# Routing table of the second layer: the slots of items 12 to 15 summed by TensorE from one-hot marks, ranks moved up, other table entries spread

## The reference

```python
gates = softmax(flat @ Wgate)                       # flat: 4096 x 256
_, top_inds = top_k(gates, 2)
mask = zeros((N, E), bool).at[arange(N)[:, None], top_inds].set(True)
pos = cumsum(mask, axis=0) * mask - 1               # rank of a token within its expert
keep = (pos < capacity) & mask
exp_in = zeros((E, capacity, d)).at[e_flat, p_eff].set(flat[t_flat], mode='drop')
hmid = gelu(einsum('ecd,edf->ecf', exp_in, W1) + b1, approximate=False)
exp_out = einsum('ecf,efd->ecd', hmid, W2) + b2
moe = zeros((N, d)).at[t_flat].add(exp_out[e_flat, p_g] * gate)
return x + moe
```

## Time and profile before

| | |
|---|---|
| median of 3 runs | 1511.07 us (1511.07 to 1511.7) |
| the profiled execution itself | 1514.36 us, of which the span from first to last instruction is 1512.6 us |
| busy in the span: PE, DVE, ACT, POOL | 1397.3, 1063.2, 898.2, 651.4 us |
| mean granted TensorE clock | 0.963 of 2.4 GHz |
| end of item 15's attention to the first product of the second layer | 1098 to 1130.7 us |
| products of the second layer | 1130.7 to the end |

### The profile page before, as it was taken

How to read it: one execution, slowest core, us unless ns; L and a number is a source line. 1 busy time by engine, 2 the same in 40 slices (tenths; PEclk the granted TensorE clock), 3 DMA queues, 4 the chain that set the end, 5 groups by cost and what they waited for, 6 DMA issues and landing times.

```text
span 1512.6 us, 26340 instructions
## 1 busy us (share of the span) xinstructions
PE 1397.3 (92%) x9265; PEld 1190.9 (79%) x9265; DVE 1063.2 (70%) x2514; ACT 898.2 (59%) x2092; POOL 651.4 (43%) x624
## 2 busy tenths in 40 slices
PE   7987899999999999999999998998729999999997
PEld 5765789999999998777876776776518888888886
DVE  2998577777777776778897787885436666666654
ACT  5776355555555553378887887887626455465452
POOL 0222344344343414555556665553434435445333
PEclk9998899999999999999999999999759999999999
DMA  6421256666665633343453454442432443234212
GB/s 176 140 81 37 60 155 170 171 177 178 172 186 170 171 102 124 100 142 116 133 147 100 135 142 102 123 123 71 126 85 58 93 102 95 38 98 100 40 22 29
DMA packets 133587, 173.53 MB, mean 115 GB/s; under 512 B 20725, under 2 KB 105536, under 8 KB 133456
## 3 DMA queue, kind: packets, MB, share of 16 engines
q1 hardware_dynamic: 105296, 119.89, 24.4%
q0 software_dynamic: 28160, 51.96, 17.3%
HBM read 107.28 MB, written 42.08 MB: 99 GB/s over the span
## 4 chain that ended last, share of the span: by engine, by line
PE 74%; DVE 8%; issue 6%; DMA 5%; ACT 3%; POOL 2%; another core or an unknown queue 1%; SPq 1%; POOLq 0%; DVEq 0%; ACTq 0%
PE banks L941 33%; PE banks L1983 8%; PE banks L1470 5%; PE banks L1514 4%; DMA xe<-pooled,idx 4%; PE banks L1985 4%; PE banks L1567 4%; PE banks L1003 3%; PE banks L451 2%; PE banks L1527 2%; PE banks L1488 1%; PE banks L1529 1%; PE banks L1959 1%; DVE row_at L516 1%
## 5 line engine op out<-in xcount | busy, mean ns | idle before, releaser
L941 PE MATMUL banks<-hi_x,hi_w 128*128 128x320 f32 (+1 forms) x832 | 289.4, 348 | 9.9 <-DVE hidden L976 5.3
L941 PE MATMUL banks<-lo_x,hi_w 128*128 128x320 f32 (+1 forms) x832 | 287.6, 346 | 0.0
L941 PE MATMUL banks<-hi_x,lo_w 128*128 128x320 f32 (+1 forms) x832 | 287.6, 346 | 0.0
L882 POOL DMA_INDIRECT xe<-pooled,idx x160 | 159.1, 995 | 235.1 <-DVE hidden L976 104.4
L1618 ACT ACTIVATE PN<-banks,smax 128x256 f32<-128x256 f32 (+1 forms) x512 | 180.3, 443 | 11.9 <-DVE smax L1724 11.9
L1443 POOL DMA_INDIRECT got<-done,slot x128 | 125.6, 981 | 143.3 <-DVE smax L1724 71.4
L1983 PE MATMUL banks<-down_w,hi_h 128*128 128x512 f32 x512 | 183.8, 401 | 0.0
L1944 POOL DMA_INDIRECT out<-X,tab x64 | 100.1, 1565 | 187.1 <-DVE X L2048 157.7
L941 PEld LDWEIGHTS banks<-hi_x,hi_w 128*128 128x128 f32 x832 | 159.6, 192 | 25.1 <-issue 8.0
L941 PEld LDWEIGHTS banks<-hi_x,lo_w 128*128 128x128 f32 x832 | 159.3, 192 | 13.7
L941 PEld LDWEIGHTS banks<-lo_x,hi_w 128*128 128x128 f32 x832 | 159.7, 192 | 12.3
(11 more groups left out here) (194 smaller groups left out, 3299.7 us busy)
## 6 DMA issues: line engine op xcount, KB each, us to landing
w<-in_L_ffn_w SPq DMA_DIRECT2D x96, 256.0 KB
done<-res SPq DMA_DIRECT2D x31, 640.0 KB
BIG<-in_L_ffn_W SPq DMA_DIRECT2D x16, 1024.0 KB
QS<-parts_qk SPq DMA_DIRECT2D x48, 256.0 KB
KS<-parts_qk SPq DMA_DIRECT2D x96, 128.0 KB
mask<-in_c_masks SPq DMA_DIRECT2D x16, 257.0 KB, 2.9
pooled<-XF SPq DMA_DIRECT2D x16, 256.0 KB, 3.2
WS<-in_L_cond_W SPq DMA_DIRECT2D x16, 256.0 KB
```

The source lines that it names most:

```text
L882: e.indirect_dma_start(xe[:, n % NXE, i, :], None, pooled, bass.IndirectOffsetOnAxis(ap=idx0[:, n * NS0 + i:n * NS0 + i + 1], axis=0)).the ...
L941: last = e.matmul(o, a[i], b[j], start=start and k == 0, stop=stop and k == 2, skip_group_check=True)
```

## The change

The 16 entries of items 12 to 15 are no longer written to DRAM. For each of these items (m = 0 to 3) a step `mark` on DVE splits its 4 times 128 slots into lane (slot / 64) and column (slot mod 64), makes one-hot marks of both and multiplies the column marks by the pair's two values; a step `find` on PE sums four products of marks into PSUM bank 0, at [lane, value, column]. The table of the other 48 entries is loaded by SP before the end of attention (`table`), to `listed`; the new `dve_table1` adds both into `tab`. To make sums possible a token is stored as a float, less N, and an empty place is 0. The slot is now place times 8 plus expert, not expert times 1024 plus place.

The ranks of group 6 (items 12, 13) and of group 7 (item 14) move up in PE's order, and their slots in DVE's. The entries of items 10 to 13's rounds that are left are spread over the rounds by waits on the count of row maxima. A load of `lanes1` (the numbers 0 to 127) is new in SP's order.

```diff
-        np.tile(np.arange(E0) * CAP0 - S0, (P, 1)), np.tile(np.arange(E1) * CAP1 - S1, (P, 1))], 1)
+        np.tile(np.arange(E0) * CAP0 - S0, (P, 1)), np.tile(np.arange(E1) - S1, (P, 1))], 1)
-    token = (p[:, None] + P * np.arange(NT)[None, :]).astype(np.int32)
+    token = p[:, None] + P * np.arange(NT)[None, :] - N
...
+        if r.stride == 1:
+            e.tensor_tensor(r.sm[:, 0:n, :], pos, base, ALU.add).then_inc(*st.next())
+        else:
+            e.scalar_tensor_tensor(r.sm[:, 0:n, :], pos, float(r.stride), base, ALU.mult, ALU.add).then_inc(*st.next())
...
     POOL_ROUND = (
         ("qk", 1, 0), ("qk", 1, 1), ("got", 3, 0, 0), ("got", 3, 0, 1), ("got", 3, 0, 2), ("entry", -3, 0), ("base", -2),
-        ("got", 3, 0, 3), ("got", 3, 1, 0), ("norm", -1, 1), ("got", 3, 1, 1), ("norm", 2, 0), ("entry", -3, 1),
+        ("late", -3, 1), ("late", -3, 2), ("late", -3, 3), ("ahead", -2, 0), ("ahead", -2, 1), ("got", 3, 0, 3), ("got", 3, 1, 0), ("norm", -1, 1), ("got", 3, 1, 1), ("norm", 2, 0), ("entry", -3, 1),
...
     POOL_LAST = (
-        *(("entry", 13, i) for i in range(TB * K1)), *(("entry", 14, i) for i in range(R * K1)), ("norm", 15, 1),
-        *(("entry", 15, i) for i in range(TB * K1)), *(("entry", 16, i) for i in range(TB * K1)))
+        ("entry", 13, 2), ("entry", 13, 3), ("norm", 15, 1))
     SP_LAST = (
-        ("base", 13), ("normed", 14), ("load_w1", 0), ("load_w1", 1), ("base", 14), ("normed", 15), ("base", 15))
+        ("lanes", 0), ("base", 13), ("normed", 14), ("load_w1", 0), ("load_w1", 1), ("base", 14), ("table", 0), ("normed", 15),
+        ("base", 15))
...
+            elif step == "table":
+                e.wait_ge(s_xc, B)
+                e.wait_ge(s_fill1, 48)
+                e.wait_ge(s_scat1, 16 * NSC)
+                e.wait_ge(s_in1, LANES_IN)
+                e.dma_start(listed, table1.rearrange("(p c) w -> p c w", p=P)).then_inc(s_in1, 16)
...
+    entry_pace = {(b, i): (s_smax, 3 * NG * (b + 3) + n) for b in range(LATE, B - 4) for i, n in ((1, 1), (2, 4), (3, 6))}
+    entry_pace.update({
+        (12, 1): (s_smax, 3 * NG * 15), (12, 2): (s_lgs, 14), (12, 3): (s_smax, 3 * NG * 15 + 1), (13, 0): (s_smax, 3 * NG * 15 + 4),
+        (13, 1): (s_smax, 3 * NG * 15 + 7), (13, 2): (s_smax, 3 * NG * 15 + 10), (13, 3): (s_smax, 3 * NG * 15 + 12)})
...
+    def pe_find1(e, m):
+        if m == 0:
+            e.wait_ge(s_pn, exp_count(NG * B - 1, 0))
+        e.wait_ge(s_marked1, m + 1)
+        for q in range(NHOT):
+            last = e.matmul(found1(), lane_hot[m % 2][:, q, :], slot_hot[m % 2][:, q, :, :].rearrange("p v c -> p (v c)"),
+                            start=m == 0 and q == 0, stop=m == 3 and q == NHOT - 1, skip_group_check=True)
+        last.then_inc(s_found1, 1)
...
+    def dve_mark1(e, m):
...
+        slots = slot1[:, t, :].rearrange("p r k -> p (r k)")
+        e.tensor_scalar(lane, slots, NCOL.bit_length() - 1, None, ALU.logical_shift_right).then_inc(*st.next())
+        e.tensor_scalar(col, slots, NCOL - 1, None, ALU.bitwise_and).then_inc(*st.next())
+        e.wait_ge(st.sem, st.n)
+        e.tensor_tensor(col_hot, wide(lanes1[:, 0:NCOL], 1, [P, NHOT, NCOL]), wide(col, 2, [P, NHOT, NCOL]),
+                        ALU.is_equal).then_inc(*st.next())
+        e.tensor_tensor(lane_hot[m % 2], wide(lanes1, 1, [P, NHOT, P]), wide(lane, 2, [P, NHOT, P]), ALU.is_equal).then_inc(*st.next())
+        e.wait_ge(st.sem, st.n)
+        e.tensor_tensor(slot_hot[m % 2], wide(col_hot, 2, [P, NHOT, 2, NCOL]),
+                        wide(pair1[:, t, :, :].rearrange("p r k v -> p (r k) v"), 3, [P, NHOT, 2, NCOL]), ALU.mult).then_inc(s_marked1, 1)
+
+    def dve_table1(e):
+        e.wait_ge(s_in1, TABLE_IN)
+        e.wait_ge(s_found1, 4)
+        found = found1().rearrange("p (v c) -> p v c", v=2)
+        flat = tab[:, :, :, :].rearrange("p i e w -> p (i e) w")
+        e.scalar_tensor_tensor(flat[:, :, 0].bitcast(U32), found[:, 0, :], float(N), listed[:, :, 0], ALU.add, ALU.add).then_inc(r1.s_slots, 1)
+        e.tensor_tensor(flat[:, :, 1], found[:, 1, :], listed[:, :, 1], ALU.add).then_inc(r1.s_slots, 1)
...
@@ sp_experts1
-        e.wait_ge(s_scat1, 16 * NT * K1)
-        e.dma_start(tab[:, :, :, :], table1.rearrange("(e p i) w -> p e i w", e=E1, p=P)).then_inc(s_tab, 16)
@@ pool_experts1
-        e.wait_ge(s_tab, 16)
+        e.wait_ge(r1.s_slots, TABLE_READY)
```

More of the change, by code:

```diff
@@ L84, in shape_constants @@
         p[:, None] + P * np.arange(NT)[None, :] - N // 2], 1)
-    token = (p[:, None] + P * np.arange(NT)[None, :]).astype(np.int32)
+    token = p[:, None] + P * np.arange(NT)[None, :] - N
     empty = np.zeros((S1, 2), np.float32)
-    empty[:, 0] = np.full(S1, N, np.int32).view(np.float32)
     f = lambda a: np.ascontiguousarray(a, dtype=np.float32)
@@ L1145, in _build @@
     QS, KS, VP = (QS0, QS1), (KS0, KS1), (VP0, VP1)
+    NHOT = TB * K1
+    NSC = NT * K1 - 4 * NHOT
+    NCOL = S1 // P
+    lanes1 = WS[:, 0, 1, 0:P]
+    lane_hot = [t.rearrange("p a b -> p (a b)").rearrange("p (q l) -> p q l", l=P) for t in (WS[:, 1, :, :], BS[:, :, :])]
+    slot_hot = [t.rearrange("p a b -> p (a b)").rearrange("p (q v c) -> p q v c", v=2, c=NCOL) for t in (x1T[:, :, :], xn[:, :, :])]
+    col_hot = hT1[:, 1, 0:NHOT * NCOL].rearrange("p (q c) -> p q c", c=NCOL)
+    listed = WS[:, 0, 1, P:P + 2 * NCOL].rearrange("p (c w) -> p c w", w=2)
+    slot_parts = [hT1[:, 0, P + i * NHOT:P + (i + 1) * NHOT].bitcast(U32) for i in range(2)]
     region.close()
-    s_attn_in = sem("attn_weights_in")
+    s_in1 = sem("second_layer_in")
     s_got0, s_ws_in = sems("results0_in", NGA * TB), sems("matrix_in", 2)
@@ L1309, in group_logits @@
         return lgs[:, t0 % R * E1:(t0 % R + n) * E1].rearrange("p (r e) -> p r e", r=n)
-    light_uses = [a for a in rounds(PE_FIRST, PE_ROUND, PE_LAST) if a[0] not in ("scores", "turn_p", "values", "tail_done")
+    light_uses = [a for a in rounds(PE_FIRST, PE_ROUND, PE_LAST) if a[0] not in ("scores", "turn_p", "values", "tail_done", "find")
                   and (a[0] != "rank" or group_ended(a[1]) is not None)]
@@ L1418, in _build @@
         (2, 4): (s_xn_turned, 2), (2, 5): (s_smax, 5), (2, 6): (s_qk_ps, 3)}
+    LATE = B - 6
+    entry_pace = {(b, i): (s_smax, 3 * NG * (b + 3) + n) for b in range(LATE, B - 4) for i, n in ((1, 1), (2, 4), (3, 6))}
+    entry_pace.update({
+        (12, 1): (s_smax, 3 * NG * 15), (12, 2): (s_lgs, 14), (12, 3): (s_smax, 3 * NG * 15 + 1), (13, 0): (s_smax, 3 * NG * 15 + 4),
+        (13, 1): (s_smax, 3 * NG * 15 + 7), (13, 2): (s_smax, 3 * NG * 15 + 10), (13, 3): (s_smax, 3 * NG * 15 + 12)})
+    spread = {a: "late" for a in entry_pace if a[0] < 13}
+    spread.update({(13, 0): "ahead", (13, 1): "ahead"})
     def pool_attn(e):
@@ L1455, in pool_attn @@
                 add_residual(e, b)
-            elif step == "entry" and entry_at(b, d[0]):
+            elif step in ("entry", "late", "ahead") and step == spread.get((b, d[0]), "entry") and entry_at(b, d[0]):
                 g, i = entry_at(b, d[0])
@@ L1461, in pool_attn @@
                     e.wait_ge(r1.s_weighted, g + 1)
+                if (b, d[0]) in entry_pace:
+                    e.wait_ge(*entry_pace[b, d[0]])
                 e.indirect_dma_start(
@@ L1600, in pe_attn @@
                 last.then_inc(s_lg1, 1)
+            elif step == "find":
+                pe_find1(e, b)
             elif step == "rank" and group_ended(b) is not None:
@@ L1803, in dve_attn @@
                 dve_slots(e, r1, group_ended(b))
+            elif step == "mark":
+                dve_mark1(e, b)
+    def dve_mark1(e, m):
+        st = dve_steps
+        t = slice(NT - 4 * TB + TB * m, NT - 4 * TB + TB * (m + 1))
+        g = NGR - 2 + max(m - 1, 0)
+        lane, col = slot_parts
+        if m == 0:
+            e.wait_ge(s_in1, LANES_IN)
+            e.wait_ge(s_xc, B)
+            e.wait_ge(s_v_ps, B)
+            e.wait_ge(s_qk_ps, TB * B)
+        if m >= 2:
+            e.wait_ge(s_found1, m - 1)
+        e.wait_ge(r1.s_slots, g + 1)
+        e.wait_ge(r1.s_weighted, g + 1)
+        if m >= 1:
+            e.wait_ge(s_marked1, m)
+        slots = slot1[:, t, :].rearrange("p r k -> p (r k)")
[15 more added lines that the diff above has]
+        e.tensor_tensor(flat[:, :, 1], found[:, 1, :], listed[:, :, 1], ALU.add).then_inc(r1.s_slots, 1)
     region = ExitStack()
```

69 lines of the change are left out of this document (41 added, 28 removed).

## The result

The changed kernel takes 1490.55 us (median of 4 runs, 1487.44 to 1493.52) against 1511.38 for the kernel before, run beside it (4 runs): ratio 0.9861, 95% interval 0.9840 to 0.9883. That is 20.8 us less where 3.85 less was forecast, and it lies outside the range. The profiled execution took 1493.52 us (span 1491.7, mean clock 0.975; before 1512.6 and 0.963).

The account below looks back on a forecast made before the run. The second layer is a solid PE block behind a hole, so starting it earlier ends it earlier. Terms -5.55 + 1.2 + 1.3 + 0.7 - 1.5 = -3.85 took 1511.07 to 1507.2 us; range 1504.6 to 1512.6.

Parts of the forecast that it names:

- Slot to gather: Item 15's slot to first gather: 11.06 us before, 5.5 after (mark, find, two sums, POOL's start), 5.55 us saved.
- Gathers beside DVE's splits: First gathers now run while DVE splits the weights: up to 0.53 us each for three gathers, taken as +1.2 us.
- Find 0: Ahead of item 15's outputs: keeps PE until 1090.3 if PE works until 1088.4, +1.3 us; otherwise 0.4.
- Find 2: Between turning XN and the gate: 1.9 us of work in a gap of 1.20, +0.7 us; bounds 0.6 and 2.6.
- the clock: PE's clock may rise during projection and find 1, speeding turning of XN, find 2 and gate: -1.5 us, ends 0 and -2.1.
- POOL's paced entries ... nothing: Entries ahead of item 14's power on POOL: the last is let go a full row maximum before the norm; no cost.
- the rival of late finds: PE's finds reach their waiters late; outputs, gate and table pay 2.1 us more each: +4.0, 1515.1 us; chance 0.11.
- Marks 0 to 2 and the earlier slots on DVE: Around item 15's last row maximum and the projection wait: moved DVE work is covered, nothing counted, at worst +1.2 us.
- more gained: Rival: find 0 costs only 0.4 us and POOL is hardly held (0.3): -5.65, 1505.4 us; chance 0.12.

Follow-up runs that it names:

- filled kernels: Changed kernel with unused identity products in PE's idle stretches: 1490.38 us, 0.9851; also with entries of items 0 to 9 moved and weight splits delayed: 1482.54, 0.9803.
- last experiment: Changed kernel with entries 1 and 2 of items 0 to 9 moved, PE's idle stretches filled, DVE's weight splits after first gather's landing: 1482.54 us, ratio 0.9803.
- second set: Runs on another chip than the first pair: kernel before 1512.69 us, changed kernel, unchanged, 1494.15 us, ratio 0.9875.
- bunched kernel: Changed kernel with its entries of items 10 to 13 not spread: 1471.76 us, 0.9938 in the first set; 1506.88 us, 0.9966 in the third set.
- third set: Runs on another chip, with spreading of entries and added table entries varied, beside the kernel before at 1511.37 us.
- first set: Runs on another chip, with parts of the change tried separately and entries held back or added, beside the kernel before at 1480.41 us.

## Why the prediction was wrong, point by point

- *Slot to gather*, forecast 11.06 to 5.5: measured 5.73. Right. (At the full clock, in the filled kernels, it is 4.8: 1090.54 to 1095.35 in the last one.)
- *Gathers beside DVE's splits*, +1.2: first to fourth gather 5.24 us instead of 3.83, +1.41. Right, and the last experiment takes it away by moving the splits (3.86, with the fourth gather longer in their place).
- *Find 0*, +1.3: the outputs start 0.83 after ACT's copy starts instead of 0.53, so +0.3. The 1.3 was read off a late ACT wait, which itself went away.
- *Find 2*, +0.7, and *the clock*, -1.5: turning XN 0.63, find 2 1.06, gate 1.03; from the start of turning XN to the start of the gate is 1.84 us instead of 2.29, the gate 0.8 shorter, together -1.3 where +0.7 and -1.5 made -0.8. Near in size, but not by the rise that I expected: in this execution the clock did not rise through find 1, it had never fallen; only find 3 ran at half speed, 2.08. That the rounds ahead had lost their idle stretches goes with it; the two were not parted. In the changed kernel of the second set the clock did fall, in the projection, and the same two terms made -0.4. In the bunched kernel of the third set, which keeps the late reports, a rise did come (projection 3.49 us, find 1 1.26), but the turning of XN was at half again (1.09).
- *"POOL's paced entries ... nothing"*: this is the step that failed. I costed moving the entries by whether anything waits for an entry. Nothing does. But the entries of the kernel before stand in runs of 4, 7 and 8, and during the run of 7 DVE starts 3.0 us (2.4 in the second set) after what it needs is over by PE's records. Spreading is worth 11.2 us, shown by the run with it alone; the sum had 0.
- The effect stood in my own text, under the rival of late finds: scores over at 1076.7, DVE at 1079.68. I took it for a fixed property of the place, asked only what it would do to the new instructions, and not what causes it and whether the change removes the cause. The right question would have put POOL's run of seven entries (back to back from 1073.20 to 1082.01 in the profile of before; the first window of the earlier trace rows has POOL busy for 4.09 of 5.70 us) beside the two late waits.
- *Marks 0 to 2 and the earlier slots on DVE*, nothing: right for the order as it is (the bunched kernel's three rounds are within 0.05 us of the kernel before), by way of the moved ranks: without these, find 2 waits 2.35 us.
- The rivals: "more gained" pointed the right way for another reason; none named the spreading. That the last stretch came out at 5.19 us where its terms made 5.15 is in part luck: slot to gather and the gathers each came out 0.2 us dearer than forecast, find 2 with the clock 0.5 us cheaper.

Left open: how PE's work comes to be late for its readers (whether the array stands still or only its signals, the records with modelled ends don't tell), whether closeness alone does it or also the place in the round where a run falls, and why the set on one chip showed none of it with the same kernels. A run with no two of POOL's indirect DMAs close together was not made.

## What to carry to other kernels

When an engine waits several microseconds for work that the records show as done, look at what the other engines issue during that wait before taking it as given, and put a cost on every edit that changes it, even if nobody waits for the moved instructions. Space out POOL's indirect DMAs, and look where the moved ones end up: runs of three and more, with gaps of 0.3 to 0.5 us, made readers of PE 1.5 to 3.7 us late on three of four chips here. Repeat an experiment on a second chip before dropping a theory: the first set alone would have buried the right one.

## What the runs showed of the hardware that was not expected

- Runs of POOL's indirect DMAs with mostly 0.30 us between them go with DVE or ACT starting 1.5 to 3.7 us after the end of PE's record (idle for 4.42, 3.72, 1.75, 0.90 us above), for gathers of 128 rows of 256 values and for table entries of 8 bytes a row alike; memsets of 3.69 us do nothing of it. In the set on one chip of four the same runs had no such waits, and the kernel before took 31 us less; between the two profiles of the bunched kernel 31 us lie in the rounds of items 5 to 15.
- In the rows above an indirect DMA of POOL takes 1.40 to 1.49 us beside DVE's sums and subtractions with two inputs in SBUF (the entry at 1077.86 among them), 1.15 or 1.16 as the first behind a power, and 0.94 to 1.02 otherwise.
- Filling idle PE time with products that nobody reads kept the clock at full: find 3 took 1.16 instead of 2.08, and the stretch to the first product 27.07 instead of 28.83, where nothing of the kernel's own work was changed.
